# The place of the norms' Newton steps in the GpSimd queue of an audio tower kernel

## The reference

```python
h = _L0_tok_ref(x)                                 # (32, 313, 128)
h = h + _L0_attn_ref(_layernorm(h, axis=-1))       # softmax(x x^T) x, per clip
h = h + _L0_ffn_ref(_layernorm(h, axis=-1), ...)
# inside the ffn, per token and per head (8 heads, two query halves of 32)
s0 = einsum('bshq,eq->bshe', _l2norm(q0), _l2norm(keys0))      # 64 scores, likewise s1
sc0, ix0 = top_k(s0, 16); sc1, ix1 = top_k(s1, 16)
cs = sc0[..., :, None] + sc1[..., None, :]; ci = ix0[..., :, None] + ix1[..., None, :]
fs, pos = top_k(cs, 16); fi = take_along_axis(ci, pos); w = softmax(fs)
act = gelu(einsum('bsd,bshkd->bshk', hidden, expert_down[fi]))
out = einsum('bshk,bshko->bso', act * w, expert_up[fi])
```

## Time and profile before

| | |
|---|---|
| runs | 2024.80, 2027.36, 2029.87 us; median 2027.36 |
| the profiled execution's own time | 2031.43 us |
| its span, first to last instruction | 2029.6 us |
| mean granted clock of PE | 0.812 of full speed |
| busy share | DVE 95%, PE 80%, POOL 71%, ACT 61% |
| transfers | 24.87 MB, 12 GB/s over the span |

### The profile page before, as it was taken

One profiled execution on the slowest core, in us unless ns is written; L12 is line 12 of the kernel. 1 busy time (PEld: TensorE's weight loads), 2 busy tenths in 40 slices (PEclk: granted clock), 3 DMA queues, 4 the chain that ended last, 5 costly groups with the idle time before them and its releaser, 6 DMA issues.

```text
span 2029.6 us, 47236 instructions
## 1 busy us (share of the span) xinstructions
PE 1632.5 (80%) x11023; PEld 1169.5 (58%) x11023; DVE 1919.0 (95%) x15718; ACT 1232.0 (61%) x3883; POOL 1433.2 (71%) x2561
## 2 busy tenths in 40 slices
PE   5577888788888888888888788888878888986667
PEld 3235566566656655665666556656656565655456
DVE  2499999999999999999999999999999999999992
ACT  3346666666666666566556766656675665665554
POOL 2247777686777767777776777777687777767775
PEclk8877888888888787888888787888888888788765
DMA  1000000000000000000000000000000000000000
GB/s 44 7 10 4 19 7 13 13 7 19 7 19 9 13 13 6 19 7 19 7 6 22 6 19 7 19 7 7 19 9 20 7 19 7 6 13 9 7 6 11
DMA packets 46669, 24.87 MB, mean 12 GB/s; under 512 B 4827, under 2 KB 46116, under 8 KB 46390
## 3 DMA queue, kind: packets, MB, share of 16 engines
q1 hardware_dynamic: 46390, 21.85, 3.9%
HBM read 11.58 MB, written 10.26 MB: 11 GB/s over the span
## 4 chain that ended last, share of the span: by engine, by line
DVE 79%; PE 11%; ACT 5%; issue 4%; POOL 1%; SPq 1%; DMA 0%; DVEq 0%; ACTq 0%
DVE idx L1071 11%; DVE idx L1078 11%; DVE hrest L1065 10%; DVE alpha L1039 10%; DVE vals L1069 7%; DVE vals L1062 7%; DVE c L1109 5%; DVE crest L1103 5%; DVE top L1106 3%; DVE top L1100 3%; PE QB L526 2%; DVE beta L1044 2%; PE FB L418 1%; PE QB L514 1%; DVE lo L1033 1%
## 5 line engine op out<-in xcount | busy, mean ns | idle before, releaser
L914 POOL TENSOR_TENSOR bw<-beta,wp 128x1024 bf16<-128x1024 bf16 x240 | 505.2, 2135 | 347.3 <-issue 171.6
L526 PE MATMUL QB<-bw,alpha 128*128 128x48 bf16 x5120 | 554.5, 277 | 106.7 <-issue 101.1
L526 PEld LDWEIGHTS QB<-bw,alpha 128*128 128x128 bf16 x5120 | 521.0, 150 | 149.2 <-issue 139.4
L749 ACT ACTIVATE WD<-QB 32x96 f32<-32x96 f32 x1280 | 307.6, 240 | 84.5 <-PE QB L526 71.6
L1039 DVE TENSOR_SCALAR alpha<-hi 128x1024 bf16<-128x1024 bf16 x640 | 274.9, 502 | 0.0
L475 PE MATMUL SC<-WK,hidT 128*128 128x512 f32 x320 | 241.0, 846 | 12.6 <-issue 11.8
L1071 DVE FIND_INDEX8 idx<-vals,sraw 128x8 uint32<-128x64 f32 x1280 | 250.6, 218 | 0.0
L1078 DVE FIND_INDEX8 idx<-vals,hrest 128x8 uint32<-128x64 f32 x1280 | 250.6, 219 | 0.0
L1065 DVE MATCH_REPLACE8 hrest<-vals,sraw 128x64 f32<-128x64 f32 x1280 | 249.6, 207 | 0.0
L1062 DVE MAX8 vals<-sraw 128x8 f32<-128x64 f32 x1280 | 169.1, 207 | 14.1 <-ACT sraw L729 14.1
L1069 DVE MAX8 vals<-hrest 128x8 f32<-128x64 f32 x1280 | 166.6, 208 | 0.0
(11 more groups left out here) (206 smaller groups left out, 3583.3 us busy)
## 6 DMA issues: line engine op xcount, KB each, us to landing
res<-h_scratch SPq DMA_DIRECT2D x80, 64.0 KB, 1.9
xin<-in_x SPq DMA_DIRECT2D x32, 128.0 KB
h_scratch<-h2n SPq DMA_DIRECT2D x32, 128.0 KB
out<-ofin SPq DMA_DIRECT2D x64, 64.0 KB, 1.5
h_scratch<-h2n SPq DMA_DIRECT2D x32, 28.5 KB
out<-ofin SPq DMA_DIRECT2D x16, 57.0 KB
xin<-in_x SPq DMA_DIRECT2D x32, 28.0 KB
xin<-in_x SPq DMA_DIRECT2D x32, 0.2 KB
```

The source lines that it names most:

```text
L526: last = mm(bank[:, 48 * u:48 * u + 48], alpha[:, buf, a, :, 8 * p + u], bwv[:, :, a, :, 8 * p + u], start=(a == 0), stop=(a == 1))
L749: last = A(WD[r, RING[(t - 4) % NT], :, 8 * p:8 * p + 8], blocks[r, :, :, g], ACT.Copy)
L914: last = tt(bw[:, buf, NY * i:NY * i + NY, :], beta[:, buf, :, :], wp[:, buf, i, :].unsqueeze(1).to_broadcast([128, NY, 256]), ALU.mult)
```

## The change

The call of `newton` for the norms of pair k leaves the begin of the second tile (p = 0, t = 1) and stands at the end of the first (p = 3, t = 0), ahead of that slot's `bw`. Nothing else is changed.

```diff
                     tt(G[:], ws[:], GL[:, :, t, :], ALU.mult).then_inc(s["g_full"], 1)
-                if p == 0 and t == 1 and exists(k, t, 0):
-                    pool.wait_ge(s["seed4_full"], k + 1)
-                    newton(y4[:], xh4[:], na[:], c15[:], s["rn_steps"], 12 * k, rn[:])
                 if p == 0 and exists(k, t, 1):
...
                     tt(Ye[:], ci[:, buf, :, :], m[:], ALU.mult).then_inc(s["y_full"], 1)
+                if p == 3 and t == 0 and exists(k, t, 0):
+                    pool.wait_ge(s["seed4_full"], k + 1)
+                    newton(y4[:], xh4[:], na[:], c15[:], s["rn_steps"], 12 * k, rn[:])
                 if p == 3 and exists(k, t, 3):
```

## The result

The changed kernel took 2030.69 us (median of 20 runs, 2028.70 to 2032.43) against 2025.94 us for the kernel before in the same series (20 runs, 2022.61 to 2029.87): ratio 1.0022, with an interval of 1.0016 to 1.0028. It is slower by 4.75 us, on the side that I forecast and inside my range, but only 0.23% and about half of the 8.5 us predicted. Later series of the very same kernel did not repeat it: 2054.65 us (one run), 2062.29 us (four) and 2069.48 us (four), beside 2025.41, 2028.74 and 2030.82 us for the kernel before: 29, 34 and 39 us slower, and outside my range. Finding out why is most of what follows.

What follows compares the result with a forecast made beforehand. DVE's instruction stream bounds the kernel. Fourteen pairs at 1.8 - 1.16 = +0.64 us give +9.0, the last pair -0.5: +8.5 us on the runs' median of 2027.36, so 2036 us, range 2025 to 2048.

Steps and rivals of the forecast that it cites:

- DVE bounds the kernel, and masks and POOL's instructions hold each other up: Whole kernel: DVE, 95% busy, sets the time; POOL's tensor instructions beside the `alpha` masks lengthen them, 2.77 to 3.90 us.
- the gain: Second tile of pairs 2 to 16: `Ye` comes earlier and leaves the masks, 15 x 1.16 = 17.4 us less.
- The price of taking turns: First tile: Newton steps beside masks cost 8 x 0.16 = 1.3 us, betas 0.5 us, together 1.8 us per pair.
- the betas: First tile: the four `beta` instructions meet three Newton steps at 0.16 us each, 0.5 us per pair.
- The last pair pays 0.65 us: Last pair: 3.35 of the steps' 5.15 us run free, some four steps meet masks, +0.65 us; net -0.5 us.
- my sum: Whole kernel: 14 pairs at +0.64 us give +9.0, the last pair -0.5, the first 0: +8.5 us.
- So all eight masks and the four betas now run beside them: First tile: Newton steps and masks both start at about 675.25, so masks and betas, 675.25 to 678.55, overlap the steps.
- my third rival: Masks at t = 0: POOL gives way until they are done, DVE pays nothing; -17.4 us, 2010 us; chance 0.08.
- What I held against it, that `cs` does enter a running row: Near the end: `cs` and `ci` enter a row of masks, 3.99 us for 2.77, so POOL is not kept out.
- PE's and ACT's work is hidden by 13.5 us of cover: Third tile: scores copied by 694.81, asked for at 708.34; this hides the later `bw`, costed at nothing.
- The rule of the Trainium skill: Two-port vector and GpSimd instructions exclude each other for the whole instruction; by it the price would be twice the forecast's.

Runs made afterwards that it cites:

- e9: The changed kernel with a wait on POOL for `lo_full` ahead of the norms' Newton steps at t = 0: 2078.64 us, ratio 1.0248.
- e6: The changed kernel with one more POOL instruction of 128x6 ahead of the norms' Newton steps at t = 0: 2065.42 us, ratio 1.0202.
- e1: The norms' 12 Newton steps left out altogether, scores scaled with the first guess `y4`, against the kernel before: 2023.23 us, ratio 0.9979.
- e2: The kernel before with a second row of 12 Newton steps of 128x80 on scratch tiles at the new place: 2059.06 us, ratio 1.0161.

## Why the prediction was right or wrong

- *DVE bounds the kernel, and masks and POOL's instructions hold each other up*: right, and the gain was right to 0.02 us a pair (17.7 us over 15 pairs in place of 17.4; the second tile goes from 3.93 to 2.76 us in the masks and from 25.2 to 24.05 us in all).
- *The price of taking turns*: the masks cost 3.96 - 2.77 = 1.2 us (I took 1.3), the betas 0.91 - 0.63 = 0.28 us (I took 0.5): 1.47 us, not 1.8. This is the term of the sum that missed in the recorded series, 14 x 0.33 = 4.6 us too much; the betas were most of it, as only two of the four met a step. Net +0.3 us a pair, not +0.64.
- *The last pair pays 0.65 us*: wrong, it paid nothing. The step that met the masks was held out. With this and the price as measured, my sum gives 14 x 0.3 - 1.16 = +3.0 us; the two tiles of the trace show +2.5 us.
- *So all eight masks and the four betas now run beside them*: this is the step that failed. They do so only in a pair whose first step gets in; elsewhere all 12 mask instructions run alone and POOL stands still. I saw that steps and masks start at the same moment and called it no accident, but did not ask what happens on either side of that moment. The mechanism of my third rival, POOL kept out of a running row of masks, is real. I gave it 0.08 and the wrong sign: it cost 3.3 to 3.6 us over a pair that takes turns, where I had it gaining 1.16 over the kernel before. What I held against it, that `cs` does enter a running row, the rows do not show: the first `cs` starts at 1971.03, 0.10 us ahead of the first mask at 1971.13, so it was running already. That the recorded series fell inside my range was luck: in its one trace the steps led by 0.07 to 0.08 us, and with 0.02 us less, as later, half of the pairs or more were held.
- *PE's and ACT's work is hidden by 13.5 us of cover*: wrong. The cover was read at the scores of the third tile. The next thing late is ACT's sum of squares for `row_seed` in that tile, with 0.06 to 0.40 us of room in the changed kernel. Its row was in the waits of before (`sv` behind `hid`, 5.6 us over four times), and I left it aside as small. With `bw` 0.5 us later this cost almost nothing, as I said (0.2 us in one pair); with `bw` 4.7 us later DVE waited 3.2 to 3.9 us in each held pair.
- *The rule of the Trainium skill* ("SBUF — State Buffer", Who interferes with whom), that the two exclude each other for a whole instruction: taking turns costs less than that (0.15 us a mask beside steps of 0.35 us), being held lasts longer (a row of 12 DVE instructions, 3.3 us). The part that says the order of issue decides, not the shape, agrees with e9, where the step that came second was held, and with e6, where six columns were held as long as 80. By the starts in the trace alone it does not hold: a step that started 0.05 us ahead was held too.
- The recorded series, with all 14 pairs taking turns in its trace, lies at +4.75 us; of it 2.5 us are the two tiles (in one profile of each kernel). Whether the rest is a real shift in the later tiles is open.

## What to carry to other kernels

Where a GpSimd instruction is moved to start together with a row of back-to-back vector instructions like these masks, compute the distance of the two starts in hundredths of a us, and cost both orders; if they are within 0.1 us, force the order with a wait or one small instruction, and time the kernel in more than one series. When work on an engine off the bound is made later, look for the smallest room in the waits of before, not for the largest cover: one that occurs in three of 14 rounds, like the 5.6 us here, marks a place with little room in all the others. A gain at one point of a pipeline whose engines run at nearly the same pace can be given back at the next meeting point, as 14.5 of 17.5 us were in e1; leave the work out altogether in one run to see how much is there.

## What was not expected of the hardware

- A GpSimd `tensor_tensor` that came after the first of 12 back-to-back DVE `tensor_scalar` on bf16 was held for all of them: 3.26 to 3.55 us for an instruction of 0.32 us, and 3.42 us for one of six columns. One that was running when the first came, and ran on for 0.13 us or more, led to turns, at 0.15 us a mask for 80 columns and 0.31 us for 160.
- In the changed kernel the border lies at 0.053 to 0.057 us between the starts (e2 has a step held at 0.060 us). The lead is used up once the POOL instruction ends within 0.09 us of the first mask's start: the next one is then held, also one of 1.3 us (`Ye`, 4.23 us).
- The same POOL instruction of 128x6 took 198 ns in some traces and 200 ns in others, nearly the same throughout a trace. In the four traces of the changed kernel this went with a run of 2031 us (198 ns) and with runs of 2055 to 2063 us (200 ns).
